# Causal attention in a four-layer kernel: scores and maxima over one head's 32 rows, the mask added by VectorE, keys and queries turned two groups ahead

## The chip, the cores and the metric

One NeuronCore of a Trainium2 chip runs the whole program. Its engines are TensorE (PE in the profile; PEld is its loading of weights), VectorE (DVE), ScalarE (ACT), GpSimd (POOL) and SyncE (SP, which here only issues transfers). The metric is the device time of one execution in microseconds, the median over several.

## The reference

The input `x` is 4 batches of 1024 tokens of 128 values. Four layers follow one another, each added to `x`: attention, a feed-forward layer with 8 experts, a second attention-like layer with a sigmoid, and the feed-forward layer again. The change is in the first:

```
k, q, v = (x @ Wk, @ Wq, @ Wv) as 16 heads of 8 values;  k, q = layernorm over the 8
dot  = einsum('bqhs,bkhs->bhqk', q, k) / sqrt(8);  dot = where(causal, dot, -inf)
attn = softmax(dot);  out = einsum('bhqk,bkhs->bqhs', attn, v) @ Wo + bo
```

## The kernel before

A batch has 8 tiles of 128 tokens, and its 16 heads are 4 groups of 4 heads. So attention is a row of 16 groups, numbered G = 4 b + g. A head has 32 rows on the partitions, four heads fill the 128. Its 8 values are stored as a rounded part and a rest, so that products of rounded numbers (fp32r) are exact enough: rows 0 to 7 and 8 to 15 of a key hold the rounded value, 16 to 23 the rest; two more rows hold ones in the keys and, in the queries, minus the maximum of the row (again as two parts); the others are zero. One matmul thus gives the score minus the maximum, and the exponential needs nothing more.

For every group there are two passes over queries times keys:

- **Maxima** (`maxima_unit` in TensorE, L704, mask L707; in VectorE L1208): queries on the partitions, up to 512 keys as columns. VectorE reduces each to one column. Where the diagonal tile is the last, a bf16 matmul of the identity with a mask adds a large negative number above the diagonal. Queries over 512 have two parts, and their two maxima are joined in `shift` (L1216). `shift` writes minus the maximum into the queries' two rows, which are then turned again (`turn_low`, `turn_high`) into `qmT`.
- **Scores** (`scores` L719; ScalarE's `weights` L894): keys on the partitions, up to 512 queries as columns. ScalarE takes the exponential into `prob`, POOL's `keep` (L1034, L1036) zeroes what lies below the diagonal of a diagonal tile, and TensorE's `weigh` (L737) multiplies with the values: four heads side by side, 128 rows by 32 columns each, into `o_acc`. ScalarE reads it out once a group (`empty_out`, L899).

In both passes the matmul is over all 128 rows. That one head alone counts is reached by `k_apart`: a copy of the turned keys for each head in which the other heads' rows are zero. SyncE's `spread` (L628) makes it with four transfers a group, after the keys `kT` are there; the zeros are written once by POOL (L254 in setup, L1105).

Everything is laid out by hand. `sequence` yields the steps of a group in one order and every engine walks the same order, doing its own part and counting the others'. Each unit of work (a score unit, a maxima unit, a turn of four tiles, a projection) takes the next of six PSUM banks in a ring: TensorE waits until the bank's last reader is through, the reader until the unit is full. A group has 38 score units and 39 maxima units. The scores are those of group G, the maxima those of G + 1: they begin in the tenth score step and end in the 37th. The steps between are placed by `PLACE`, a list of 24 score numbers. Queries of G + 1 are turned at its start and emptied by VectorE (L1258), keys of G + 2 near its end and emptied by ScalarE (L888). Group 1 of a batch also projects the next batch (L686), group 2 normalises its keys and queries (POOL's `square` and `affine`, L998 to L1008), group 0 finishes the batch before. In the last five groups come steps of the feed-forward layer's routing, and POOL sends rows by indirect transfers (`send`, L1068) in the last two.

The opening makes the first batch's projections, turns the first keys and queries, and runs all maxima of group 0 with nothing beside them.

## Time and profile before

| | us |
|---|---|
| median of the timed runs | 2882.5 (2881.8 to 2883.1) |
| profiled execution: span from first to last instruction | 2834.4 |
| what lies around the span, if that execution took the median | 48.1 |
| attention's groups: first maximum, last reading of `o_acc` | 42.5, 724.3 |
| one plain group (198.3 to 234.0) | 35.7 |
| a group that projects the next batch (278.9 to 320.9) | 42.0 |
| a group that normalises it (320.9 to 360.5) | 39.6 |
| mean granted TensorE clock | 0.97 |

The profiled execution is known by its span; 48.1 us is the median less the span. A group is measured from one reading of `o_acc` (L899) to the next, sixteen in all. Two matmuls may overlap: the duration of one (its mean ns) holds the way through the array, and the time from one start to the next is what a stream of them costs. Busy time counts overlapping instructions once.

### The profile page before, as it was taken

How to read it: one execution, taken by the hardware profiler on the slowest of the kernel's cores; microseconds unless marked ns; L12 is line 12 of the kernel's file. 1: busy time of each engine (PE TensorE's matmuls, PEld its weight loads, DVE VectorE, ACT ScalarE, POOL GpSimd, SP SyncE). 2: the span in 40 equal slices, each digit the busy share in tenths (PEclk: the TensorE clock that was granted, in tenths of full speed). 3: DMA queues.
4: the chain of work that ended last, by engine and by line, in shares of the span. 5: the costliest groups of instructions: out<-in, count | busy, mean ns of one | idle time of the engine just before them, and what ended most of it. 6: DMA issues, size and time to landing. Idle time of an engine off the chain costs nothing. (4 is left out here: it accounts for less than half of the span.)

```text
span 2834.4 us, 54508 instructions
## 1 busy us (share of the span) xinstructions
PE 2635.7 (93%) x19182; PEld 1713.2 (60%) x19182; DVE 1789.9 (63%) x3491; ACT 1578.4 (56%) x2843; POOL 820.0 (29%) x1181
## 2 busy tenths in 40 slices
PE   5999998998689979999999999999999999996997
PEld 3555565655478845666555665555555555554886
DVE  7777777786466745555665556555556655555666
ACT  2666666666454455555555556555566555554443
POOL 4142422525345311111111111112121123322642
PEclk8999999999799979999999999999999999997998
DMA  6500000001424258888878888887888788885222
GB/s 109 82 16 16 8 16 16 16 9 31 119 83 157 94 130 196 195 196 196 204 184 200 196 196 189 190 187 177 188 189 190 183 201 200 206 199 203 71 87 85
DMA packets 190430, 383.21 MB, mean 135 GB/s; under 512 B 45281, under 2 KB 100714, under 8 KB 188810
## 3 DMA queue, kind: packets, MB, share of 16 engines
q1 hardware_dynamic: 181578, 362.55, 53.9%
q0 software_dynamic: 8640, 17.84, 1.8%
q8 instruction: 132, 2.16, 0.4%
q14 instruction: 80, 0.66, 0.1%
HBM read 38.10 MB, written 39.86 MB: 28 GB/s over the span
## 5 line engine op out<-in xcount | busy, mean ns | idle before, releaser
L3050 DVE STREAM_TRANSPOSE m_turned<-m_sig 128x1024 f32<-128x1024 f32 x512 | 613.6, 1227 | 429.5 <-ACT m_sig L2820 201.1
L2643 PE MATMUL m_v_ps<-m_sig,m_tok 128*64 128x512 f32 x2048 | 468.2, 599 | 0.0
L2656 PE MATMUL m_v_ps<-m_sigT,m_tok 128*64 128x256 f32 x4064 | 461.5, 380 | 3.2 <-DMA m_sigT<-m_turned 3.2
L1208 DVE TENSOR_REDUCE a_maxima<-a_bank 128x1 f32<-128x512 f32 (+4 forms) x624 | 367.4, 643 | 121.1 <-PE a_bank L707 73.2
L2627 PE MATMUL m_f_ps<-m_swap,m_own 64*128 64x512 f32 x1536 | 426.2, 404 | 15.6 <-DMA m_swap<-m_own 7.4
L894 ACT ACTIVATE a_prob<-a_bank 128x512 f32<-128x512 f32 (+1 forms) x608 | 322.2, 586 | 201.0 <-PE a_bank L719 197.5
L2627 PE MATMUL m_f_ps<-m_own,m_swap 64*128 64x512 f32 x1536 | 426.4, 404 | 0.0
L2656 PEld LDWEIGHTS m_v_ps<-m_sigT,m_tok 128*64 128x64 f32 x4064 | 289.4, 137 | 200.3 <-issue 54.8
L2916 POOL TENSOR_TENSOR m_own<-m_uv,m_own 128x1024 fp32r<-128x1024 f32 x64 | 152.0, 2375 | 813.4 <-ACT m_own L2782 813.4
L2820 ACT ACTIVATE m_sig<-m_f_ps 128x1024 f32<-128x1024 f32 x256 | 248.3, 1022 | 245.4 <-issue 147.5
L2627 PEld LDWEIGHTS m_f_ps<-m_swap,m_own 64*128 64x128 f32 x1536 | 271.6, 186 | 99.9 <-ACT m_sig L2806 25.8
L2643 PEld LDWEIGHTS m_v_ps<-m_sig,m_tok 128*64 128x64 f32 x2048 | 135.8, 137 | 265.3 <-issue 265.0
L719 PE MATMUL a_bank<-a_qmT,k_apart 128*128 128x512 f32 (+3 forms) x768 | 266.0, 407 | 25.0 <-DVE a_maxima L1208 11.6
L2806 ACT ACTIVATE m_sig<-m_f_ps 128x512 f32<-128x512 f32 x512 | 264.2, 603 | 41.0 <-PE m_f_ps L2627 39.3
L2627 PEld LDWEIGHTS m_f_ps<-m_own,m_swap 64*128 64x128 f32 x1536 | 271.4, 186 | 5.6
L704 PE MATMUL a_bank<-k_apart,a_qT 128*128 128x512 f32 (+3 forms) x768 | 249.2, 386 | 26.2 <-DVE a_maxima L1208 11.6
L2832 ACT CAST m_v1T_hi<-m_v_ps 128x256 fp32r<-128x256 f32 x128 | 47.7, 372 | 276.9 <-PE m_v_ps L2656 272.5
L719 PEld LDWEIGHTS a_bank<-a_qmT,k_apart 128*128 128x128 f32 x768 | 131.5, 197 | 97.9 <-issue 64.0
L704 PEld LDWEIGHTS a_bank<-k_apart,a_qT 128*128 128x128 f32 x768 | 146.6, 202 | 61.9 <-DVE a_maxima L1208 24.4
L3059 DVE TENSOR_TENSOR m_v1T_lo<-m_v_ps,m_v1T_hi 128x256 fp32r<-128x256 f32 x128 | 54.2, 424 | 204.5 <-ACT m_v1T_hi L2832 204.3
L737 PE MATMUL a_o_acc<-a_prob,v 128*32 128x512 f32 (+3 forms) x1536 | 147.4, 501 | 9.6 <-POOL a_prob L1036 7.5
L1827 PE MATMUL f_y_ps<-f_w_down,f_innerT 128*128 x1136 | 150.3, 275 | 1.4 <-DVE f_y_rows L2237 1.1
(509 smaller groups left out, 4268.6 us busy)
## 6 DMA issues: line engine op xcount, KB each, us to landing
m_sigT<-m_turned SPq DMA_DIRECT2D x2042, 128.0 KB, 2.3
m_swap<-m_own SPq DMA_DIRECT2D x64, 256.0 KB, 3.2
f_t_rows<-f_sent_rows SPq DMA_DIRECT2D x142, 65.0 KB, 2.1
f_sent_rows<-a_proj SPq DMA_DIRECT2D x34, 260.0 KB, 9.5
k_apart<-a_kT SPq DMA_DIRECT2D x64, 128.0 KB, 2.4
m_swap<-m_own SPq DMA_DIRECT2D x64, 128.0 KB, 3.2
f_h<-back_rows SPq DMA_DIRECT2D x8, 512.0 KB, 5.6
rows<-back_rows SPq DMA_DIRECT2D x6, 512.0 KB, 4.9
```

The costliest lines, as they stand in the source:

```text
L704: mm = pe.matmul(out[:, i, :], qT[g % 2][:, qt * P:(qt + 1) * P], k_apart[g % 2][:, h + i, k0:k1], start=(i == 0 or not masked), stop=not ...
L719: mm = pe.matmul(out[:, i, :], k_apart[g % 2][:, h + i, j * P:(j + 1) * P], qmT[g % 2][:, q0:q1], start=True, stop=True)
L894: act.activation(prob[j % 2][:, h:h + heads, prob_cols(j, q0, q1)], src, ACT.Exp).then_inc(u.free(), 1)
L1208: dve.tensor_reduce(maxima[:, qt, h:h + heads, part], src, AX.X, ALU.max).then_inc(u.free(), 1)
L1827: mm = pe.matmul(y_ps[:, 0:DIM], innerT[p][:, ib * P:(ib + 1) * P], w_down[:, ds(e * INTER + ib * DIM, DIM)], start=(ib == 0), stop=(ib == ...
L2627: mm = pe.matmul(f_ps[s][:, cols], tile_of(u[rows, :], j + s * SIDE), v[rows, cols], start=start, stop=stop)
L2643: mm = pe.matmul(v2_ps[h * RANK:(h + 1) * RANK, :], tok[p][:, 0, j + s * SIDE, :], sig[j % 2][s][:, h * HALF:(h + 1) * HALF], start=(j == ...
L2656: mm = pe.matmul(v1_ps[h * RANK:(h + 1) * RANK, g * 2 * P:(g + 1) * 2 * P], tok[p][:, 1, jj, :], sigT[g][:, :, 2 * h:2 * h + 2, jj, :].rea ...
L2806: ins = act.activation(sig[1][s][:, cols], f_ps[s][:, cols], ACT.Sigmoid)
L2820: act.activation(sig[j % 2][s][:, :], f_ps[s][:, :], ACT.Sigmoid).then_inc(sig_ready, 1)
L2916: pool.tensor_tensor(own_lo[p][:, :], uv32[:, :], own_hi[p][:, :].bitcast(F32), ALU.subtract).then_inc(lo_ready, 1)
L3050: dve.transpose(turned[g][:, :, q, :, :], sig[j % 2][s][:, :].rearrange("p (t j a) -> p j t a", j=4, a=STACK)).then_inc(turn_ready, 1)
```

## The change

- `k_apart`, its clearing and its transfers go. Scores and maxima read the 32 rows of one head straight from `kT`, `qT` and `qmT`, so each matmul is 32 rows by 128 columns. A unit holds one head's pieces, one or two tiles' worth; unit n of the scores has head n mod 4, of the maxima (n + 2) mod 4.
- The mask matmuls go. `mask` is 128 x 512 in fp32, zero but for its last 128 columns, and VectorE's `tensor_tensor_reduce` adds it and takes the maximum in one instruction, with the first part's maximum (`first_max`) as its start value. It also writes the masked scores, into four buffers that nobody reads.
- Keys are kept in three buffers, and both keys and queries are turned two groups ahead, near a group's end. ScalarE empties them and `qmT`'s second half, where VectorE did.
- 40 score units and 40 maxima units; maxima run from the first score step to the 38th. `PLACE` is gone, the steps are placed by score numbers. `prob` is laid out by a table, and two diagonal tiles share a unit in two places.

```diff
-        SCORES, MAXES = list(score_units()), list(max_units())
+        SCORE_PIECES = (((0, 0, HALF),), ((1, P, HALF),), ((0, HALF, SEQ),), ((1, HALF, SEQ),), ((2, 2 * P, HALF), (3, 3 * P, HALF)),
+                        ((2, HALF, SEQ),), ((3, HALF, SEQ),), ((4, 4 * P, SEQ),), ((5, 5 * P, SEQ),), ((6, 6 * P, SEQ), (7, 7 * P, SEQ)))
+        MAX_PIECES = (((0, 0, P), (1, 0, 2 * P)), ((2, 0, 3 * P),), ((3, 0, HALF),), ((4, 0, HALF),), ((5, 0, HALF),),
+                      ((4, HALF, 5 * P), (5, HALF, 6 * P)), ((6, 0, HALF),), ((6, HALF, 7 * P),), ((7, 0, HALF),), ((7, HALF, SEQ),))
+        SCORES = [(pieces, h) for pieces in SCORE_PIECES for h in range(GROUP)]
+        MAXES = [(pieces, (h + GROUP // 2) % GROUP) for pieces in MAX_PIECES for h in range(GROUP)]
-        WEIGHED_AFTER = {LAST_OF[1]: (0,), LAST_OF[2]: (1,), LAST_OF[3]: (2,), LAST_OF[4]: (3,), LAST_OF[6]: (4, 5)}
+        WEIGHED_AFTER = {15: (0,), 20: (1,), 27: (2,), 32: (3,), 36: (4,), 39: (5,)}
...
         def sequence(g, prev, prep, follows, stage=None):
-            begin, end, made = PLACE[4], 36, 0
-            if prev and follows:
-                yield "spread", 0
+            two_ahead, first = prep or g < HALVES_OF, follows and not prev
+            begin, end, made = 6 if first else 0, 37, 0
...
+                if two_ahead and i in (31, 32, 34, 35):
+                    yield ("keys", "queries")[i // 34], (31, 32, 34, 35).index(i) % HALVES_OF
...
+                if prep and g == 2 and i in (0, 2, 5, 7, 9, 10, 12, 20, 21):
+                    yield {0: ("square", 1), 2: ("square", 0), 5: ("square_sums", 0), 7: ("head_dev", 0), 9: ("head_rstd", 0),
+                           10: ("affine", 1), 12: ("stack_keys", 0), 20: ("affine", 0), 21: ("stack_queries", 0)}[i]
...
         @block.tensor
+            def maxima_unit(u, G, n, stacks=()):
+                pieces, h = MAXES[n]
+                out, rows, col = u.next(), head_rows(h), 0
                 u.wait_empty(pe, *stacks)
-                if n == 0:
-                    pe.wait_ge(k_spread, 16 * GROUP * (G + 1))
-                for i in range(heads):
-                    mm = pe.matmul(out[:, i, :], qT[g % 2][:, qt * P:(qt + 1) * P], k_apart[g % 2][:, h + i, k0:k1], start=(i == 0 or not masked), stop=not masked)
-                if masked:
-                    mask = k["mask"][:, :].unsqueeze(1).broadcast_to([P, heads, P])
-                    mm = pe.matmul(out[:, :, k1 - k0 - P:k1 - k0], k["ident16"][:, :], mask, start=False, stop=True)
+                for qt, k0, k1 in pieces:
+                    mm = pe.matmul(out[:, col:col + k1 - k0], qT[G % 2][rows, qt * P:(qt + 1) * P], kT[G % KEPT_KEYS][rows, k0:k1], start=True, stop=True)
+                    col += k1 - k0
                 mm.then_inc(unit_full, 1)
...
-                for i in range(heads):
-                    mm = pe.matmul(out[:, i, :], k_apart[g % 2][:, h + i, j * P:(j + 1) * P], qmT[g % 2][:, q0:q1], start=True, stop=True)
+                for j, q0, q1 in pieces:
+                    mm = pe.matmul(out[:, col:col + q1 - q0], kT[G % KEPT_KEYS][rows, j * P:(j + 1) * P], qmT[G % 2][rows, q0:q1], start=True, stop=True)
...
         @block.vector
+            def maxima_unit(u, n, firsts_made, masked_by):
+                pieces, h = MAXES[n]
+                src, col = u.next(), 0
                 u.wait_full(dve)
-                dve.tensor_reduce(maxima[:, qt, h:h + heads, part], src, AX.X, ALU.max).then_inc(u.free(), 1)
+                masks = any(k1 == (qt + 1) * P for qt, _, k1 in pieces)
+                if masks:
+                    masked_by.append(u.n)
+                    if len(masked_by) > MASKED_OUTS:
+                        u.wait_emptied(dve, masked_by[-1 - MASKED_OUTS])
+                for qt, k0, k1 in pieces:
+                    width = k1 - k0
+                    scores, first = src[:, col:col + width], first_max[:, qt % HALF_T, h:h + 1]
+                    masked = masked_out[(len(masked_by) - 1) % MASKED_OUTS][:, col:col + width]
+                    col += width
+                    if k1 < (qt + 1) * P:
+                        ins = dve.tensor_reduce(first, scores, AX.X, ALU.max)
+                        firsts_made[qt, h] = u.n
+                        continue
+                    if k0:
+                        u.wait_emptied(dve, firsts_made[qt, h])
+                    ins = dve.tensor_tensor_reduce(out=masked, in0=scores, in1=k["mask"][:, HALF - width:HALF], scale=1.0,
+                                                   scalar=first if k0 else MASKED, op0=ALU.add, op1=ALU.max, accum_out=maxima[:, qt, h:h + 1])
+                ins.then_inc(u.free(), 1)
```

## Rows read from the trace of the kernel before

**Rows 1.** The page's first part: busy us, share of the span, instructions of each engine.
```profile
PE 2635.7 (93%) x19182; PEld 1713.2 (60%) x19182; DVE 1789.9 (63%) x3491; ACT 1578.4 (56%) x2843; POOL 820.0 (29%) x1181
```
**Rows 2.** Table of stretches: length, busy us (instructions) by engine, clock, DMA share, GB/s.
```profile
42.00:70.00 28.00, 22.38 (x89) 14.18 (x89) 24.94 (x45) 2.22 (x3) 14.50 (x19) 0.80 1.10 157
70.00:695.80 625.80, 580.56 (x3902) 362.94 (x3901) 474.10 (x997) 393.81 (x764) 213.01 (x384) 0.97 0.12 23
278.90:320.90 42.00, 41.60 (x276) 26.20 (x274) 27.09 (x52) 27.23 (x62) 7.41 (x18) 0.98 0.06 13
320.90:360.50 39.60, 36.80 (x249) 22.40 (x249) 31.10 (x56) 25.10 (x47) 24.98 (x32) 0.96 0.06 14
360.50:396.10 35.60, 33.90 (x240) 20.70 (x238) 26.42 (x50) 22.12 (x43) 9.09 (x24) 1.00 0.07 16
617.40:661.80 44.40, 38.55 (x252) 23.07 (x251) 38.07 (x103) 28.00 (x60) 6.42 (x17) 0.96 0.06 13
695.80:724.30 28.50, 18.86 (x138) 8.74 (x137) 1.00 (x4) 15.06 (x30) 20.96 (x32) 0.88 0.12 38
```
**Rows 3.** Groups by line and shape, 198.3 to 234.0: count, busy us, mean ns, idle before.
```profile
L1208 DVE TENSOR_REDUCE a_maxima<-a_bank 128x1 f32<-128x512 f32 x24 | 15.1, 684 | 4.3 <-PE a_bank L704 2.5 <-PE a_bank L707 1.8
L1208 DVE TENSOR_REDUCE a_maxima<-a_bank 128x1 f32<-128x384 f32 x8 | 4.3, 555 | 0.6 <-PE a_bank L707 0.5
L1258 DVE CAST a_qT<-a_bank 128x512 fp32r<-128x512 f32 x2 | 1.3, 684 | 1.4 <-PE a_bank L668 1.4
```
**Rows 4.** Stretch 198.3 to 234.0 of L1208, L707 and L737 alone, in this order.
```profile
198.30:234.00 35.70, 22.97 (x40) 1.00 0.07 16
198.30:234.00 35.70, 5.82 (x24) 2.26 (x24) 1.00 0.07 16
198.30:234.00 35.70, 8.98 (x96) 2.46 (x96) 1.00 0.07 16
```
**Rows 5.** TensorE in order of time, around 300 us: start, us, instruction.
```profile
299.75 0.40 PE L704 MATMUL a_bank<-k_apart,a_qT 128*128 128x512 f32 x1
300.08 1.50 PE L737 MATMUL a_o_acc<-a_prob,v 128*32 128x256 f32 x16
...
303.37 0.39 PE L719 MATMUL a_bank<-a_qmT,k_apart 128*128 128x512 f32 x1
303.60 0.60 PE L668 MATMUL a_bank<-ident,k_st 128*128 128x128 f32 x4
...
304.25 0.48 PE L719 MATMUL a_bank<-a_qmT,k_apart 128*128 128x512 f32 x1
304.57 0.34 PE L704 MATMUL a_bank<-k_apart,a_qT 128*128 128x384 f32 x1
```
**Rows 6.** TensorE in order of time at 1500 us, the second attention layer's 64-row matmuls.
```profile
1500.57 0.39 PE L2627 MATMUL m_f_ps<-m_swap,m_own 64*128 64x512 f32 x1
1500.57 0.39 PE L2627 MATMUL m_f_ps<-m_own,m_swap 64*128 64x512 f32 x1
1500.81 0.39 PE L2627 MATMUL m_f_ps<-m_swap,m_own 64*128 64x512 f32 x1
```
**Rows 7.** VectorE: five reductions in order of time; then groups of the whole span.
```profile
213.23 3.08 DVE L1208 TENSOR_REDUCE a_maxima<-a_bank 128x1 f32<-128x512 f32 x5 [0.84 <-PE a_bank L704]
...
L2280 DVE TENSOR_TENSOR f_inner<-f_silu,f_up 128x512 f32<-128x512 f32 x142 | 97.7, 688 | 39.5 <-PE f_up L1805 20.7 <-ACT f_silu L1958 15.8 <-PE f_out L1814 2.4
L2246 DVE SCALAR_TENSOR_TENSOR x<-f_h,ratio,x 128x128 f32<-128x128 f32 x32 | 11.0, 343 | 0.0
L2237 DVE COPY f_raw<-f_y_ps 128x128 f32<-128x128 f32 x96 | 27.9, 291 | 39.3 <-PE f_y_ps L1827 37.8 <-issue 0.6
```
**Rows 8.** Setup and the opening in order of time.
```profile
8.08 3.54 POOL L255 MEMSET k_st<- 128x4096 f32 x1
8.20 3.44 DVE L90 TENSOR_SCALAR a_spread<-a_spread 128x8 f32<-128x8 f32 x1
...
38.06 0.59 ACT L888 CAST a_qT<-a_bank 128x512 fp32r<-128x512 f32 x1 [0.27 <-PE a_bank L668]
...
41.57 0.66 PE L704 MATMUL a_bank<-k_apart,a_qT 128*128 128x128 f32 x2 [3.54 <-DMA k_apart<-a_kT]
```

More of the change, by code:

```diff
@@ L341, in attention_phase @@
     HEAD_STAGES, EARLY_UNITS = 5, 12
+    KEPT_KEYS, MASKED_OUTS = 3, 4
     with ExitStack() as ctx, ExitStack() as phase:
@@ new lines, in sequence @@
+                if prev and i == 17:
+                    for n in range(HALVES_OF):
+                        yield "turn_out", n
+                if prev and g == 0 and i in (23, 29):
+                    for n in range(HALVES_OF):
+                        yield ("turn_tokens", "project_out")[i == 29], n
+                if prep and g == 1:
+                    if i in (1, 3, 5):
+                        yield ("token_stats", "token_dev", "token_norm")[i // 2], 0
+                    if i in (13, 15):
+                        yield "turn_z", i // 15
+                    if i in (21, 23, 26, 29):
+                        for n in range(2):
+                            yield "project", 2 * (21, 23, 26, 29).index(i) + n
@@ L554, in sequence @@
+                if prev and g == 0 and 32 <= i <= 36:
+                    yield ("add_x", 0) if i == 32 else ("out_stats", i - 33)
+                if follows and i == 21:
+                    yield "turn_low", 0
                 if stage is not None:
@@ L599, in head_rows @@
             return slice(h * STACK, (h + 1) * STACK)
-        def by_head(bank, width, heads):
-            return bank[:, 0:heads * width].rearrange("p (i w) -> p i w", w=width)
         def half_of(tile, n):
@@ L890, in weights @@
             def weights(u, n):
-                j, h, heads, q0, q1 = SCORES[n]
-                src = by_head(u.next(), q1 - q0, heads)
+                pieces, h = SCORES[n]
+                src, width = u.next(), sum(q1 - q0 for _, q0, q1 in pieces)
+                to, off = prob_of(*pieces[0][0:2])
+                start = pieces[0][1] - off
                 u.wait_full(act)
-                act.activation(prob[j % 2][:, h:h + heads, prob_cols(j, q0, q1)], src, ACT.Exp).then_inc(u.free(), 1)
+                act.activation(to[:, h, start:start + width], src[:, 0:width], ACT.Exp).then_inc(u.free(), 1)
             def empty_out(G):
@@ L1387, in early_table, with group @@
                 dve.tensor_scalar(k["early_expert"][:, :], expert_sum[0:1, :], -1.0, None, ALU.add)
[L1389 to L1391 removed]
+            def group(u, link, b, g, prev, prep, follows, masked_by, head_made=()):
+                ahead, projected, firsts_made = (g + 1) % GROUPS, [], {}
                 for what, n in sequence(g, prev, prep, follows, stage_of(b, g)):
                     if what == "max":
[L1394 to L1395 removed]
+                        made = maxima_unit(u, n, firsts_made, masked_by)
+                    elif what == "next_keys":
+                        keep_turned(u, half_of(kT[(GROUPS * b + ahead) % KEPT_KEYS], n))
+                    elif what == "next_queries":
                         keep_turned(u, half_of(qT[ahead % 2], n))
[L1397 to L1401 removed]
                     elif what == "shift":
@@ L1411, in group @@
                         out_stats(b - 1, n)
-                    elif what in ("score", "keys", "turn_low", "turn_tokens", "turn_z", "project"):
+                    elif what in ("score", "keys", "queries", "turn_low", "turn_high", "turn_tokens", "turn_z", "project"):
                         u.next()
```

255 lines of the change are left out of this document (81 added, 174 removed).

## The prediction

> **What bounds the kernel now.** I read the page's first part first: TensorE is busy 93% of the span, VectorE 63%, ScalarE 56% [rows 1]. That is a mean over stages, so the table of stretches comes next. The change touches attention alone, and attention's pipeline of sixteen head groups runs from 42 us (first maximum) to 724 us (last reading of the output bank). Between 70.0 and 695.8 us TensorE is busy 580.6 of 625.8 us (0.93), VectorE 474.1 (0.76), ScalarE 393.8 (0.63) [rows 2]. The reader is to see there that TensorE is the full engine in attention, but that VectorE stands only 107 us behind it: whatever is taken from TensorE brings gain only until VectorE is full. Two stretches are different. In the opening (42 to 70 us) there are only maxima, and VectorE is busy 24.9 of 28.0 us (0.89). In the last group (695.8 to 724.3) there are no maxima, VectorE is idle, and POOL has 21.0 of 28.5 us, its row transfers standing between the diagonal masks for which the weighing waits [rows 2].
>
> Third, one plain group, 198.3 to 234.0 us, by line and by shape. It takes 35.7 us. VectorE's maxima cost 22.97 us of it, the mask matmuls 5.82 us, the weighing 8.98 us [rows 4]; a maximum over 512 columns takes 684 ns, over 384 columns 555 ns, an eviction by VectorE 684 ns [rows 3].
>
> **The change, part by part.**
>
> Mask matmuls out of TensorE. 23 units a group end in one, 5.82 us of busy time [rows 4]. Part of that lies beside neighbours; on the other hand a 512-column matmul behind one is followed after 0.32 us (304.25 to 304.57) and without one after 0.23 us (303.37 to 303.60) [rows 5]. I take 5.0 us a group.
>
> Scores and maxima over 32 rows. Their columns are as many as before: 2 x 18,432 a group (4 heads x 4,608), or 72 matmuls' worth of 512 columns, at 0.23 us each 16.6 us [rows 5]. Neighbouring units use different 32-row strips. The trace has no 32-row strips, but it has 64-row ones: two matmuls of 64 x 512 start together and the next two 0.24 us later [rows 6], so a pair costs what one costs. Bounds for the 16.6 us: no overlap (0 saved) and four at once (12.4 saved). I take half, 8.3 us, the row being pairs.
>
> Changes of shape. A weighing (128 x 32) that follows a 512-column matmul starts 0.33 us after it, instead of 0.23 [rows 5]: about 0.1 us a change. The turns (128 x 128), eight or more a group, now stand between 32-row matmuls, so up to 16 changes more, plus the lost overlap: +1.8 us (bounds 0 and 4). The Trainium skill (TensorEngine Tiling (Array Packing), Key Properties) says that a change of tiling mode drains TensorE; the trace's 0.1 us agrees, and without a price on the page the sum goes by the row.
>
> TensorE in all, over the 15 groups of the long stretch: 580.6 - 15 x 5.0 + 15 x 1.8 - 15 x 8.3 = 408 us. It stops being the bound.
>
> VectorE's maxima. Columns stay (18,432), instructions go from 39 to 48 a group, 16 plain and 32 that add the mask from SBUF, take the maximum and write both. Start to start a 512-column reduction costs (3.08 - 0.69) / 4 = 0.60 us [rows 7], and by 129 ns for 128 columns [rows 3] about 0.08 us of that doesn't depend on width. Nine more instructions are +0.7 us, less what the by-unit busy count already holds of gaps: +0.4. The masked form is not in this trace. From below: a two-input sum of 512 columns with one input in PSUM takes 688 ns, as the reduction does (0 more); one with an operand read per partition takes 343 ns against 291 for a copy of the same 128 columns (+0.05) [rows 7]. From above: half rate, worked out as a rival. I take +0.055 us for 32 instructions, 1.8 us. The maxima become 22.97 + 0.4 + 1.8, near 25.2 us. The Trainium skill (VectorE: DVE Perf Modes, Two Vector instructions with no wait between them) says that an instruction which also writes its accumulator is two, the second a read of the accumulator; no run here shows it, and it would put the addition above my value, by the cost of a small instruction.
>
> Evictions moved. Two of qT and one of qmT go from VectorE to ScalarE: -3 x 0.60 = -1.8 us for VectorE, +3 x 0.59 [rows 3, 8] for ScalarE. The maximum of the two parts over 16 columns goes too (-0.2). VectorE's sum: +2.2 - 2.0, nothing. ScalarE has 393.8 + 15 x 2 = 424 us and stays third.
>
> Order. Maxima now run from the first score to the 38th, where they began at the tenth; VectorE's idle stretch at the head of a group goes. What is late next is VectorE itself, and then TensorE's bursts: a weighing of about 1.5 us [rows 5] lets VectorE's share of the six banks (three, 1.8 us of work) run dry for about 0.7 us, four times a group. Keys and queries two groups ahead are waited for in good time, except in the group that normalises the next batch, where POOL has 25 us of work [rows 2] (a rival).
>
> The spread. 64 transfers and the wait for them go. They cost where nothing else runs: once, in the opening. The last cast of the queries ends at 38.65 us and the first maximum's matmul starts at 41.57 [rows 8]: -2.9 us. Against it the opening's maxima, which are VectorE's, take 2.2 us more. In setup the cleared 4,096 columns of POOL go. VectorE's tiny instruction L90 lasts 3.44 us, exactly beside POOL's second clearing (8.08 to 11.62 us), and ScalarE waits for it [rows 8]. That clearing starts at 4.9 now: -3.0 us, with 0.3 for the wider mask counted.
>
> **Sum.** What share can VectorE reach when it is the bound? 0.89 in the opening, where nothing disturbs it, and 0.857 in the stretch from 617.4 to 661.8 us, where TensorE has nearly as much to do [rows 2]. I take 0.87: 474 / 0.87 = 545 us. The three groups that project the next batch (as 278.9 to 320.9 [rows 2]) don't get there: TensorE has 41.6 - 5.0 + 1.8 - 8.3 = 30.1 us, ScalarE 29, so 33.5 instead of 31.1: +7. Together 552 against 625.8: -74. The last group is POOL's: 0. Opening -0.7, setup -3.0. Nothing behind attention changes. Total -78 us of the execution's 2834.4 us span; the timed runs have a median of 2882.5, 48 us more, for what lies around the span, and I carry the difference over: 2805 us.
>
> **Rivals.**
> Masked maxima at half rate (slower). 10,240 of a group's columns go through the masked form; at 1.01 ns each [rows 3] half rate costs 10.3 us a group instead of 1.8. VectorE: 474 + 15 x 8.5 = 602 us; at a share of 0.91 (between 0.89 and TensorE's 0.93 now) 661 us, 35 over today's, and with the opening's 8.5 - 0.7 and setup's -3 about +40: 2922 us. It decides from the point where VectorE's group grows by (625.8 x 0.87 - 474) / 15 = 4.7 us, 0.2 us per masked instruction. Against it: every two-input row of the trace runs at full rate [rows 7]. The Trainium skill (Vector Engine (DVE) Microarchitecture Reference, Points that are easy to get wrong) names half throughput for an accumulating form with two wide SBUF sources; here one source is PSUM. Chance 0.09.
>
> Strips don't overlap. TensorE then has 533 us; at 0.93 that is 573, with VectorE at 0.83 beside it rather 578: -48, so 2831 us. Rows 6 speak against it. Chance 0.13.
>
> The clock. Where TensorE is not full it is granted less: mean 0.80 in the opening, 0.88 in the last group, 1.00 in a full group [rows 2]. At 0.88 its 408 us become 464, still under VectorE's, but every burst is longer, some 1.5 us a group: -55, 2828 us. Chance 0.14; that it stays at half for good, and TensorE becomes the bound again at 816 us, 0.02 (far slower), since a full TensorE is shown at full clock.
>
> POOL late in the group of 25 us of work (its diagonal masks stand behind its scaling steps): 3 us in three batches, 2814 us. Chance 0.08.
>
> **Numbers.** Forecast 0.54, rivals as given. Lower end: VectorE at TensorE's share of today, 474 / 0.93 = 510, -119: 2764. Upper end: the rivals of 2828 and 2831 together, 2855. Half rate is left out. What a measurement tells from no change is 0.2%, 6 us. Faster 0.87 (all but half rate and the dead clock), slower 0.11, same 0.02 (a price near 0.2 us per masked instruction).
>
> **What would show it.** Groups of 30 to 31 us where they took 35.7, VectorE at 0.87 or more there and TensorE under 0.8; the masked form at 0.65 us for 512 columns start to start; pairs of 32-row matmuls starting within a few ns of each other after a weighing; a mean clock near 1 in full groups; the first maximum about 6 us earlier. A masked form above 0.8 us, or a clock below 0.9, would make it wrong.

## The result and the profile after

The changed kernel takes 2941.2 us (median of five; 2907.5 to 2947.5) against 2881.8 us for the kernel before in the same session: 1.019 times the time, 95% interval 1.014 to 1.024. It is slower by about 59 us where 77 us less were forecast, and outside the range. Four of the five runs lie at 2940 to 2947 us; the profiled one is the fifth, of 2907.5 us (span 2905.7). A second set, taken later, gave 2924.8 us and a ratio of 1.014 [1.009, 1.019], with a profiled span of 2931.5 us; its trace is called after2 below. The two sets differ in size, not in sign.

The page's first part for the kernel after, and three rows of its second (the span in 40 slices), against [rows 1]:

```profile
PE 2671.1 (92%) x18814; PEld 1641.2 (56%) x18814; DVE 1784.2 (61%) x4087; ACT 1597.3 (55%) x2918; POOL 811.9 (28%) x1179
...
PE   6988998999678979999999999999999999996897
...
DVE  7677677667364755555665556555556655556556
...
PEclk7688877767899989999999999999999999997998
```

TensorE has 368 instructions fewer and yet 35 us more busy time, and it is still the full engine in attention (the first ten slices). What has changed there is the third line: 6 to 8 tenths of the full clock, where the long stretch before had 0.97 [rows 2].

Stretches of the kernel after (columns as in rows 2): up to the last read of the attention's output; the opening; a plain group; then three stretches at a single level of the clock.

```profile
0.00:756.60 756.60, 668.36 (x3816) 325.15 (x3816) 526.31 (x1704) 446.05 (x907) 259.10 (x457) 0.76 0.11 20
...
36.00:70.00 34.00, 28.68 (x79) 16.07 (x79) 28.64 (x89) 5.52 (x10) 16.84 (x22) 0.55 1.25 181
...
207.20:243.00 35.80, 34.48 (x226) 15.81 (x224) 26.28 (x89) 23.11 (x48) 8.86 (x24) 0.86 0.00 1
...
613.40:657.60 44.20, 42.41 (x187) 21.27 (x185) 29.38 (x96) 24.40 (x47) 12.26 (x23) 0.50 0.00 1
252.00:278.50 26.50, 25.37 (x188) 14.02 (x186) 22.97 (x79) 17.61 (x37) 6.54 (x18) 1.00 0.01 1
463.50:493.50 30.00, 29.45 (x198) 14.61 (x190) 18.80 (x64) 20.81 (x51) 5.48 (x13) 1.00 0.01 2
```

In 613.4 to 657.6 us the granted clock is at its lower level (1.2 of 2.4 GHz) throughout, while TensorE is busy 42.41 of 44.20 us. "Busy" doesn't mean "at full clock". The trace of the kernel before has such a stretch too, though short: TensorE busy all the time, at the lower level.

```profile
328.13:331.54 3.41, 3.41 (x17) 1.24 (x9) 2.21 (x2) 1.31 (x3) 0.00 (x0) 0.50 0.00 0
```

A clock of 0.76 over 756.6 us, with only two levels, is (1 - 0.76) x 2 x 756.6 = 363 us at the lower one; summed from the trace's own record it is 365.1 us, against 70.6 us before the last read in the kernel before (its second profile, before2 below). The sum over all stretches of the kernel after at the upper level, from 70.0 to 728.4 us:

```profile
sum 347.19, PE 332.43 PEld 173.83 DVE 263.94 ACT 243.67 POOL 114.25; mean PE 17.50 PEld 9.15 DVE 13.89 ACT 12.82 POOL 6.01
```

So even at full clock TensorE is busy 0.96 of the time and VectorE 0.76. The forecast had under 0.8 for the one and 0.87 for the other.

The next rows are groups of TensorE's instructions in the stretch 252.0 to 278.5 us (upper level):

```profile
L640 PE MATMUL a_bank<-a_qmT,a_kT 32*128 32x512 f32 x16 | 5.5, 493 | 0.2
L627 PE MATMUL a_bank<-a_kT,a_qT 32*128 32x512 f32 x13 | 4.9, 446 | 0.0
L660 PE MATMUL a_o_acc<-a_prob,v 128*32 128x512 f32 x32 | 4.2, 595 | 0.0
```

and these the same three in 613.4 to 657.6 us (lower level): 754, 779 and 1030 ns for 446, 493 and 595.

```profile
L627 PE MATMUL a_bank<-a_kT,a_qT 32*128 32x512 f32 x17 | 11.3, 754 | 1.1 <-DVE a_maxima L1155 1.0
L640 PE MATMUL a_bank<-a_qmT,a_kT 32*128 32x512 f32 x17 | 10.3, 779 | 0.0
L660 PE MATMUL a_o_acc<-a_prob,v 128*32 128x512 f32 x40 | 9.1, 1030 | 0.0
```

VectorE's work is as forecast. By shape, 207.2 to 243.0 us (the answer to rows 3 and 4):

```profile
L1150 DVE TENSOR_REDUCE a_first_max<-a_bank 128x1 f32<-128x512 f32 x16 | 10.3, 684 | 4.8 <-PE a_bank L627 4.7
L1155 DVE CUSTOM_DVE_ANT_0 a_masked_out<-a_bank,mask 128x512 f32<-128x512 f32 x5 | 3.2, 685 | 0.0
L1155 DVE CUSTOM_DVE_ANT_0 a_masked_out<-a_bank,mask,a_first_max 128x512 f32<-128x512 f32 x4 | 2.9, 750 | 1.0 <-PE a_bank L627 1.0
L1155 DVE DVE_READ_ACCUMULATOR2_ANT a_maxima<- 128x1 f32 x32 | 2.6, 83 | 0.0
```

The masked form runs at the plain reduction's rate (685 against 684 ns for 512 columns); the read of the accumulator behind it costs 83 ns, the start value read per partition 65 ns. All the maxima of the group are 25.0 us, against 22.97 before [rows 4]: the stretch by VectorE's instructions of L1150 alone, then of L1155 alone.

```profile
207.20:243.00 35.80, 10.29 (x16) 0.86 0.00 1
...
207.20:243.00 35.80, 14.72 (x65) 0.86 0.00 1
```

The setup and the opening of the kernel after in order of time (before: L90 3.44 us, first matmul of a maximum at 41.57 us, [rows 8]):

```profile
8.52 0.34 DVE L90 TENSOR_SCALAR a_spread<-a_spread 128x8 f32<-128x8 f32 x1
...
36.62 0.67 PE L627 MATMUL a_bank<-a_kT,a_qT 32*128 32x128 f32 x10 [0.77 <-ACT a_qT L814]
...
38.05 0.23 DVE L1155 CUSTOM_DVE_ANT_0 a_masked_out<-a_bank,mask 128x128 f32<-128x128 f32 x1
```

### The profile page after: what moved, and what is told of

It reads as the page before. It is cut to its first block and busy times, and to the rows that moved or that the text cites. A ratio compares the mean times of both kernels' runs of the same rounds, so it can differ in the third digit from the quotient of the medians.

```text
span 2905.7 us, 54730 instructions
## 1 busy us (share of the span) xinstructions
PE 2671.1 (92%) x18814; PEld 1641.2 (56%) x18814; DVE 1784.2 (61%) x4087; ACT 1597.3 (55%) x2918; POOL 811.9 (28%) x1179
## 5 line engine op out<-in xcount | busy, mean ns | idle before, releaser
L2573 PE MATMUL m_f_ps<-m_swap,m_own 64*128 64x512 f32 x1536 | 426.0, 404 | 16.6 <-DMA m_swap<-m_own 8.4
L627 PE MATMUL a_bank<-a_kT,a_qT 32*128 32x512 f32 (+3 forms) x768 | 277.6, 496 | 31.8 <-DVE a_maxima L1155 20.2
L640 PE MATMUL a_bank<-a_qmT,a_kT 32*128 32x512 f32 (+3 forms) x768 | 247.0, 501 | 25.9 <-DVE a_maxima L1155 13.2
L1150 DVE TENSOR_REDUCE a_first_max<-a_bank 128x1 f32<-128x512 f32 x256 | 165.1, 684 | 91.8 <-PE a_bank L627 89.4
L640 PEld LDWEIGHTS a_bank<-a_qmT,a_kT 32*128 32x128 f32 x768 | 112.4, 220 | 167.5 <-issue 110.5
L660 PE MATMUL a_o_acc<-a_prob,v 128*32 128x512 f32 (+3 forms) x1536 | 198.1, 639 | 5.9 <-POOL a_prob L968 3.6
L627 PEld LDWEIGHTS a_bank<-a_kT,a_qT 32*128 32x128 f32 x768 | 138.1, 226 | 108.4 <-DVE a_maxima L1155 50.2
L3005 DVE TENSOR_TENSOR m_v1T_lo<-m_v_ps,m_v1T_hi 128x256 fp32r<-128x256 f32 x128 | 54.2, 423 | 217.0 <-ACT m_v1T_hi L2778 205.6
L1773 PE MATMUL f_y_ps<-f_w_down,f_innerT 128*128 x1136 | 153.3, 278 | 25.8 <-DVE f_raw L2183 17.9
```

The source lines that it names most:

```text
L627: mm = pe.matmul(out[:, col:col + k1 - k0], qT[G % 2][rows, qt * P:(qt + 1) * P], kT[G % KEPT_KEYS][rows, k0:k1], start=True, stop=True)
L640: mm = pe.matmul(out[:, col:col + q1 - q0], kT[G % KEPT_KEYS][rows, j * P:(j + 1) * P], qmT[G % 2][rows, q0:q1], start=True, stop=True)
L660: mm = pe.matmul(o_acc[h * STACK:(h + 1) * STACK, q0:q1], v1[:, j, g * GROUP + h, :], weights_at[:, h, q0 - off:q1 - off], start=(j == 0), ...
L1150: ins = dve.tensor_reduce(first, scores, AX.X, ALU.max)
L1773: mm = pe.matmul(y_ps[:, 0:DIM], innerT[p][:, ib * P:(ib + 1) * P], w_down[:, ds(e * INTER + ib * DIM, DIM)], start=(ib == 0), stop=(ib == ...
L2573: mm = pe.matmul(f_ps[s][:, cols], tile_of(u[rows, :], j + s * SIDE), v[rows, cols], start=start, stop=stop)
```

## The experiments

All the numbers are from the table; the text under each heading says what it decides. "Last read" is the start of the last copy of the attention's output bank. "Lower level" is the time before it that the trace's record of the granted clock has at 1.2 GHz. "Rest" is the last read less half of the lower level: the time that would be left if everything in those stretches ran twice as fast. It is an estimate and a lower bound, since VectorE's and ScalarE's work doesn't. "Pairs" counts, between 70 and 760 us, a scores and a maxima matmul that follow one another in order of time and start within 20 ns of each other, of some 1,480 such matmuls. Two scores or two maxima matmuls are not counted. In onestrip and fill2 the attention ends later, so that the count covers a part of it, and fill2's takes in its added matmuls. Ratios are to the kernel before in the same session, with 95% intervals.

```
kernel      median us  ratio                  last read  lower level  rest   pairs
before2     2875.0     (one run)               726.3       70.6      691.0     0
after       2941.2     1.019 [1.014, 1.024]    756.6      365.1      574.0   307
after2      2924.8     1.014 [1.009, 1.019]    785.3      419.3      575.6   310
rows128     2840.9     0.987 [0.985, 0.988]    693.2       95.6      645.4     0
rows64      2883.9     1.002 [1.001, 1.003]    733.1      215.0      625.6   226
fill2       3010.9     1.046 [1.044, 1.048]    857.6      331.9      691.7   385
samestrip   2890.4     1.004 [1.002, 1.006]    739.8      340.7      569.4   367
alldiffer   2872.8     0.998 [0.996, 0.999]    722.4      290.2      577.3   489
onestrip    3059.4     1.064 [1.062, 1.067]    902.7      587.1      609.2     0
pairs       2875.1     0.999 [0.998, 1.000]    728.5      218.2      619.4   257
twice       2873.3     0.999 [0.997, 1.000]    719.3       61.4      688.6     0
apart2      2868.1     0.996 [0.994, 0.997]    718.4       90.2      673.3     0
apartb      2840.5     0.986 [0.984, 0.987]    694.0       75.1      656.5     0
```

**rows128**: the changed kernel with all 128 rows in every scores and maxima matmul.

```diff
-                out, rows, col = u.next(), head_rows(h), 0
+                out, rows, col = u.next(), slice(0, P), 0
...
-                link(dve.tensor_scalar(hi.bitcast(F32R), maxima[:, mine, :], -1.0, None, ALU.mult))
+                link(dve.tensor_scalar(hi.bitcast(F32R), maxima[:, mine, :], -0.25, None, ALU.mult))
```

(The first edit stands in `maxima_unit` and in `scores`, the second in both instructions of `shift`. rows64 is edited at the same places, onestrip at the first alone. All three leave out that the heads are kept apart: they time the same instructions, but don't compute the attention.)

> The changed kernel, but scores and maxima read all 128 rows (the four heads' scores are summed, and minus a quarter of the maximum stands in each head, so the softmax stays in range; the heads are not kept apart, that part of the computation is changed). Instructions, columns, banks and order are those of the changed kernel; only the rows of 80 matmul units a group differ. Clock theory (a matmul over 32 rows does not keep TensorE's clock up): mean granted clock of 0 to 760 us back from 0.76 to 0.94 or more, plain groups 32 to 34 us, 2800 to 2840 us in all. Rival (what costs is the changes of shape and the drains between 32-row and 128-column work): also faster, but by 1.6 us a group, to about 2880 us, with the clock still under 0.85. Rival (VectorE's masked maxima are the cost): no change, 2905 to 2945 us.

Measured: 2840.9 us, 84 to 100 us under the changed kernel's two sets, with columns, units, waits and VectorE's instructions as they were. Its row up to the last read:

```profile
0.00:693.20 693.20, 613.25 (x3816) 384.43 (x3816) 525.54 (x1704) 447.73 (x906) 260.36 (x457) 0.93 0.11 21
```

VectorE has the same 526 us as in the kernel after; the clock is 0.93 instead of 0.76. So VectorE isn't what lost the time. TensorE was idle as much in both, 48 of 596 us here and 57 of 658 us in the kernel after (70 us to the last read but one), so that gaps in its work don't tell the two apart either.

**rows64**: the same with the rows of two heads.

```diff
+                out, rows, col = u.next(), slice(h // 2 * 2 * STACK, (h // 2 * 2 + 2) * STACK), 0
```

> As before it, but each matmul reads the 64 rows of two heads (two heads' scores summed, minus half of the maximum in each). Clock theory, if what counts is the rows in use: clock between those of 32 and 128 rows, 0.85 to 0.93 in attention, 2830 to 2890 us; it keeps the overlap of two strips, so it could also equal 128 rows. Shape rival: like 32 rows, 2905 to 2945 us, since a 64-row matmul changes the shape as often.

Measured: 2883.9 us, 215 us at the lower level: between 32 and 128 rows in both. With 32, 64 and 128 rows in use the lower level has 365, 215 and 96 us. A 64-row matmul changes the array's shape as often as a 32-row one, so the rival of the changes of shape doesn't account for the 150 us between them.

**fill2**: an extra matmul of 128 rows and 512 columns ahead of every second maxima unit.

```diff
+                if n % 2 == 0:
+                    pe.matmul(out[:, 0:HALF], qT[G % 2][:, pieces[0][0] * P:(pieces[0][0] + 1) * P], kT[G % KEPT_KEYS][:, 0:HALF], start=True, stop=True)
```

> The changed kernel with work added: before every second maxima unit one matmul of 512 columns over all 128 rows, into the same bank, overwritten by the unit's own. 20 a group, at 0.23 us and two changes of shape (0.1 us each) 8.6 us a group at full clock. Clock theory: the clock in attention rises to 0.9 or more, and the kernel with more work is faster than without, 2840 to 2900 us. Shape and VectorE rivals: the added work is paid, +60 to +130 us, 2990 us or more.

Measured: 3010.9 us. The 320 fillers took the lower level down by 33 us only (365 to 332) and put 118 us into the rest (574 to 692), 0.37 us each. Full-row work bought for its own sake costs more than the clock gives back. The clock theory's forecast (a clock of 0.9 or more in attention, 2840 to 2900 us) failed: the share of the time at the lower level fell from 0.48 to 0.39 only. The time that came is the one its rivals had named, 2990 us or more. The rows in use thus move the clock the way the theory says, but no run gives a rule for how much.

**samestrip**: the heads of the maxima in another order.

```diff
-        MAXES = [(pieces, (h + GROUP // 2) % GROUP) for pieces in MAX_PIECES for h in range(GROUP)]
+        MAXES = [(pieces, h) for pieces in MAX_PIECES for h in range(GROUP)]
```

> The changed kernel with the maxima's heads in the scores' order, so that a score unit and the maxima unit beside it use the same 32 rows and cannot overlap; four neighbours of one kind still differ. If overlap of strips carries much of the time (the prediction took 8.3 us a group): 20 us or more above the changed kernel. If banks come free one by one and TensorE is late only in bursts: within 15 us of it.

Measured: 2890.4 us, 34 to 51 us faster than the changed kernel. The premise was wrong: in the order of the steps, scores unit n is followed by maxima unit n + 1 in the first half of a group and n + 2 in the second, and then by scores unit n + 1. So in the changed kernel's order (h + 2) a maxima unit has the strip of the scores unit ahead of it in the second half, and in this order that of the scores unit behind it in the first: each order has one neighbour on the same strip in one half. This one came out with more overlaps (367 against 307), not none; why more isn't shown. Two places of the kernel after, where the strips are the same (0.33 us apart) and where they differ (together):

```profile
299.86 0.49 PE L640 MATMUL a_bank<-a_qmT,a_kT 32*128 32x512 f32 x1
300.19 0.39 PE L627 MATMUL a_bank<-a_kT,a_qT 32*128 32x128 f32 x2
...
532.94 0.79 PE L627 MATMUL a_bank<-a_kT,a_qT 32*128 32x512 f32 x1
532.94 0.68 PE L640 MATMUL a_bank<-a_qmT,a_kT 32*128 32x384 f32 x1
```

**before2**: no edit.

> The kernel before once more, for a second trace of it. Its first profiled execution had a span of 2834.4 us, while the timed ones lay at 2873 to 2882; the 44 us between them would lie in what follows the attention, 2110 us there and 2146 to 2151 us in the five other kernels' traces. If the first profile was one short execution: this one shows a span near 2878, its last read of the attention's output near 724 us, and some 2150 us behind it. If instead a profiled execution of this kernel always runs short: a span near 2834 again, and 2110 us behind.

Measured: span 2873.2 us, last read 726.3. What follows the last read, in the profile that the prediction was read from and in this one:

```profile
724.30:2834.40 2110.10, 1996.44 (x14998) 1314.36 (x14998) 1260.75 (x2383) 1154.65 (x2012) 552.33 (x722) 0.97 0.70 171
```

```profile
726.30:2873.20 2146.90, 2000.65 (x14998) 1312.91 (x14998) 1257.57 (x2383) 1150.55 (x2012) 552.38 (x722) 0.98 0.68 168
```

The first profiled execution was a short one, by 37 us, all but 2 of it behind attention with the same instructions. The twelve other traces of the study have 2146 to 2153 us there. A timed run is 1.8 us above its span, not the 48 us that the prediction carried over as lying around the span.

**onestrip**: every scores and maxima matmul on the rows of head 0.

```diff
+                out, rows, col = u.next(), head_rows(0), 0
```

> The changed kernel with every scores and maxima matmul on the rows of head 0 (the heads are not kept apart, so what is computed is not the attention asked for; columns, units and all waits are as in the changed kernel). No two neighbours are ever on different strips, so none overlap. Theory (TensorE's clock follows how many rows are in use at a time, and half of the pairs overlapped before): less work at a time, so the clock stays at its lower level for longer than the changed kernel's 365 us, and the overlaps are gone: at full clock 8.3 us a group more, at half 16.6; 15 groups at 8 to 20 us more make 3060 to 3200 us. Rival (the overlap is too seldom to matter and the clock is already set by one strip's rows): within 20 us of the changed kernel's 2941.

Measured: 3059.4 us, just under the theory's 3060 to 3200, and no overlaps. The row up to the last read:

```profile
70.00:902.70 832.70, 806.17 (x3682) 462.61 (x3681) 488.43 (x1555) 452.36 (x862) 231.42 (x413) 0.67 0.01 4
```

TensorE is busy 97% of the stretch and the clock is at 0.67, the lowest of the study: with matmuls of 32 rows one at a time the lower level came oftener than with those that overlap. The rival (within 20 us of 2941) is out.

**alldiffer**: maxima and scores beside each other on different strips all through a group.

```diff
+        MAXES = [(pieces, (h + (i < 5)) % GROUP) for i, pieces in enumerate(MAX_PIECES) for h in range(GROUP)]
```

> The changed kernel with the heads' order of the maxima such that a maxima unit and the scores unit beside it are on different strips all through a group (in the changed kernel only in the first half; the order alone is changed). Theory (rows in use at a time): 16 more pairs a group overlap, 4 us a group at full clock, and the clock keeps its upper level longer: 2850 to 2900 us, and less than 300 us at the lower level before the attention's last read. Rival (what differs between orders is chance in where the lower stretches fall): between 2890, the one other order run so far, and 2941.

Measured: 2872.8 us, 489 pairs, 290 us at the lower level. One line of order takes 52 to 68 us off the changed kernel and brings it to the time of the kernel before, a little under it. The rest is the same in samestrip, after and alldiffer (569 to 577 us); what differs is the lower level. So of the theory's two parts one failed: 182 more pairs than in the kernel after took nothing off the rest, where 4 us a group were expected, and all of the gain came by the clock.

**apart2**: the changed kernel's order of work and its masking, with the former matmuls over 128 rows.

```diff
-    KEPT_KEYS, MASKED_OUTS = 3, 4
+    KEPT_KEYS, MASKED_OUTS = 2, 4
-            begin, end, made = 6 if first else 0, 37, 0
+            begin, end, made = 9, 37, 0
...
+                    mm = pe.matmul(out[:, col:col + k1 - k0], qT[G % 2][:, qt * P:(qt + 1) * P], k_apart[G % 2][:, h, k0:k1], start=True, stop=True)
...
+                    ins = dve.tensor_tensor_reduce(out=scores, in0=scores, in1=k["mask"][:, HALF - width:HALF], scale=1.0,
```

> The changed kernel's order of work, its masking within VectorE's maximum and its turns two groups ahead, but with the kernel before's matmuls over all 128 rows (keys spread to two zeroed buffers by SP at a group's start; maxima begin at step 9 of 40, since the buffer is only then free and filled; VectorE writes the masked scores back to their bank, and the mask is in bf16). The full attention is computed. Theory (the 32-row matmuls alone cost the time; the rest of the change is worth what rows128 showed, 39 us): 2835 to 2860 us, the clock at its lower level for about 100 us of the attention, a group without projections at 31 to 35 us. Rival (the maxima all through a group were what made rows128 fast, and begun at step 9 they queue on VectorE): 2865 to 2885 us.

Measured: 2868.1 us, in the rival's range (2865 to 2885) and outside the theory's. The clock is as the theory had it, 90 us at the lower level. Here three quarters of the rows of each key buffer are zero, as in the kernel before: rows of zeros kept the clock up as other rows did. Part of the time is a price that I had added: with the masked scores written back to their bank, and the mask in bf16, the read of the accumulator takes 144 ns instead of 83.

```profile
L1190 DVE DVE_READ_ACCUMULATOR2_ANT a_maxima<- 128x1 f32 x480 | 68.9, 144 | 0.0
L1190 DVE CUSTOM_DVE_ANT_0 a_bank<-a_bank,mask,a_first_max 128x512 f32<-128x512 f32 x60 | 43.0, 756 | 4.0 <-PE a_bank L667 3.9
L1190 DVE CUSTOM_DVE_ANT_0 a_bank<-a_bank,mask 128x512 f32<-128x512 f32 x60 | 41.1, 722 | 19.7 <-PE a_bank L667 19.6
```

**pairs**: matmuls over two heads' 64 rows, one head's zeroed, on three spread buffers, in alldiffer's order.

```diff
+        def pair_rows(h):
+            return slice(h // 2 * 2 * STACK, (h // 2 + 1) * 2 * STACK)
...
+                    sp.dma_start(k_apart[G % APARTS][rows, h % 2, :].bitcast(F32), kT[G % KEPT_KEYS][rows, :].bitcast(F32)).then_inc(k_spread, 16)
```

> The changed kernel with scores and maxima over two heads' 64 rows, the other head's rows zeroed (SP spreads each group's keys to one of three buffers of two slots, right after they are turned, four DMAs of 128 KB that took 2.4 us each in apart2), and the heads' order of alldiffer, so that most neighbouring units stand on different halves of the rows and can overlap. Masking, turns two groups ahead and maxima all through a group stay; the full attention is computed. Theory (the time is the work at full clock, which overlapping shortens, plus half of what is spent at the lower level, which more rows in use shorten): alldiffer spent 290 us at the lower level before the attention's last read, rows64 215, rows128 96; with overlapping pairs of 64 rows under 180, and the work at full clock between alldiffer's 577 and rows64's 626 us; 2810 to 2850 us. Rival (64-row matmuls on different halves don't overlap, as rows64's time suggests): 2870 to 2890, rows64's 2884. Other rival (the spread of keys lands too late for maxima that begin with the group): 1 to 3 us a group more than the theory.

Measured: 2875.1 us. Halves do overlap (257 pairs), but hardly oftener than in rows64 (226), and the lower level has the same 218 us. The first maximum comes at 42.6 us, as before the change. The forecast of 2810 to 2850 failed: the pairs that the order should bring didn't come, and the lower level stayed over the 180 us expected. The time lies in the first rival's range (2870 to 2890), but its reason doesn't hold, since halves do overlap. Why there are few pairs isn't shown. TensorE waited for the spread once between 70 and 700 us, for 1.1 us, so the other rival is out.

**twice**: rows128 with TensorE's mask matmul put back; the heads are not kept apart here either.

```diff
+                    if masked:
+                        mm = pe.matmul(out[:, col - P:col], k["ident16"][:, :], k["mask16"][:, :], start=False, stop=True)
```

> rows128 (scores and maxima over all 128 rows, the clock near full) with TensorE's mask matmul put back in every masked piece of a maxima unit, 32 of 128 columns a group, while VectorE masks as well (masking twice changes nothing): the mask matmuls' price on TensorE by itself. Theory (my sum took 5.0 us a group for them, TensorE being the bound): 16 groups at 4 to 5 us, 2905 to 2921 us against rows128's 2841. Rival (TensorE waits for VectorE's maxima in rows128, so the matmuls fit beside): under 20 us more, below 2861.

Measured: 2873.3 us, 32 us over rows128. The mask matmuls have 110.1 us of busy time, 7.3 us a group, but TensorE's busy time grew by 34 us only: the remainder of each lies beside a neighbour. The answer is between the theory (64 to 80) and the rival (under 20). With the mask matmuls the lower level is shorter, 61 us against 96. The group, then the stretch of twice and that of rows128:

```profile
L634 PE MATMUL a_bank<-mask,ident 128*128 128x128 bf16 x477 | 110.1, 233 | 0.0
```

```profile
70.00:719.30 649.30, 600.63 (x4152) 369.13 (x4151) 475.00 (x1552) 435.20 (x859) 232.18 (x413) 0.97 0.02 5
```

```profile
70.00:693.20 623.20, 566.71 (x3668) 353.26 (x3667) 471.72 (x1544) 428.19 (x857) 231.91 (x412) 0.95 0.02 5
```

**apartb**: apart2 with three places mended.

```diff
-    KEPT_KEYS, MASKED_OUTS = 2, 4
+    KEPT_KEYS, MASKED_OUTS = 2, 3
-            begin, end, made = 9, 37, 0
+            begin, end, made = 5, 37, 0
+        masked_out = [sb(f"a_masked_out{i}", [P, HALF], BF16) for i in range(MASKED_OUTS)]
-        o_tokT = sb("a_o_tokT", [P, SEQ])
+        o_tokT = oT
-            pool.memset(k["k_apart0"][:, :, :].bitcast(F32), 0.0)
+            for i in range(2):
+                pool.memset(k[f"k_apart{i}"][:, :, :].bitcast(F32), 0.0).then_inc(other_cleared, 1)
```

(The last edit moves the clearing from the setup to POOL's part behind it. The mask is in f32 again, too.)

> apart2 (128-row matmuls on spread keys, masking in VectorE, turns two groups ahead; the full attention) with three places mended: VectorE writes the masked scores to a buffer of 512 bf16 columns in SBUF instead of back to their bank (in apart2 the read of the accumulator behind it took 144 ns against 83 in the changed kernel, and the 512-column form 722 against 685: about 3 us of VectorE a group), the two 3.5 us clearings of the key buffers stand behind the setup on POOL (apart2's first maximum came at 42.6 us, the changed kernel's at 38.2), and the maxima begin at step 5 instead of 9. Theory (each of these was on the path): 4.4 us at the opening and 0.5 to 1.3 us in each of 15 groups, so 2845 to 2857 us, the attention's last read near 700. Rival (only TensorE's work and clock count, 673 us of work at full clock in apart2): the opening's 4 us alone, 2862 to 2866. Other rival (the spread, 2.4 us and its issue, is late for step 5): 2868 or more.

Measured: 2840.5 us, 0.986 [0.984, 0.987] of the kernel before and 2.9% under the changed one (2924.8 in the same session), with the whole attention computed: the version that beats both. It came out 5 us under the theory. The edits came together, so what each is worth isn't shown, and with them stays open how much of apart2's time was the late start of the maxima, its rival's cause. Two groups of VectorE by shape:

```profile
L1197 DVE DVE_READ_ACCUMULATOR2_ANT a_maxima<- 128x1 f32 x480 | 39.6, 82 | 0.0
L1197 DVE CUSTOM_DVE_ANT_0 a_masked_out<-a_bank,mask 128x512 bf16<-128x512 f32 x60 | 38.4, 686 | 1.9 <-PE a_bank L667 1.5
```

and the long stretch:

```profile
70.00:694.00 624.00, 568.24 (x3690) 354.18 (x3688) 470.18 (x1557) 432.86 (x864) 232.90 (x415) 0.96 0.12 25
```

The accumulator's read is back at 82 ns, the clock at 0.96, near the 0.97 before the change [rows 2].

**after2**: no edit, beside the same runs of before as apartb.

> The changed kernel once more, beside the same runs of the kernel before: its first profile was of an execution of 2907 us, while its timed ones lay at 2940 to 2947. Theory (where the lower clock falls decides, and it falls differently from one execution to the next): the time at the lower level before the attention's last read comes out other than 365 us by about twice the difference in time; an execution of 2940 would show near 430. Rival (the executions differ in what follows the attention, as those of the kernel before did): the last read near 757 us again, and more behind it.

Measured: span 2931.5 us, 25.8 over the first profile, and the last read is 28.7 us later with 54.2 us more at the lower level, 0.53 us each. What follows the last read is 2146 us against 2149. Nor is it these two alone: in the nine timed runs of the changed kernel the mean granted clock is 0.920 in the two shortest and 0.906 to 0.909 in the five longest, and span times clock, the time that two levels leave at full clock, is 2661 to 2678 us, while the spans go from 2906 to 2946. Most of the changed kernel's spread is the spread of its time at the lower level.

## Why the prediction was wrong

**The step that failed: the clock, put at nothing "since a full TensorE is shown at full clock".** The prediction gave the clock two cases: 2828 us at 0.88 (0.14), and "that it stays at half for good, and TensorE becomes the bound again at 816 us, 0.02 (far slower), since a full TensorE is shown at full clock". That reason was read from rows in which every scores and maxima matmul had 128 rows, and it was a mean: the stretch from 328.13 to 331.54 us, shown above, is full and at the lower level. The changed one's have 32, and in 613.4 to 657.6 us TensorE is full and at the lower level. What happened lies between the two cases: mean clock 0.76, or 0.73 in after2. The price by the table: the lower level grew from 71 to 365 us, (365 - 71) / 2 = 147 us, against 117 us won in the rest (691 to 574): +30, which is the last read's 726.3 to 756.6. Between its two cases the prediction had given the clock no chance. That the rows in use are the cause is shown by the edits to the rows alone (rows128, rows64, onestrip) and that overlap matters by the edits to the order alone (samestrip, alldiffer). How it comes about in the chip, and how many rows are enough, stay open. The Trainium skill (TensorE: Matmul & The Clock Gate, HAM oscillation) puts such changes of clock down to gaps in TensorE's work. The kernel before agrees: seven of the eight falls of its clock between 70 us and the last group came in or just behind a gap of 2.2 us or more. In the kernel after only two of eighteen did, and a stretch of 44.2 us at the lower level has TensorE busy 96%; there the measurement decides.

**TensorE's 408 us: "it stops being the bound".** This failed too, apart from the clock. Busy time at the upper level plus half of that at the lower, between 70 us and the last read but one, is 467 us in the kernel after against 563 in before2: an estimate of the work at full clock. 96 us went, where the prediction took 580.6 - 408 = 172. From 252.0 to 278.5 us VectorE does reach 0.87, the share that the forecast gave it as the bound, but from 463.5 to 493.5 us, at full clock as well, it has 18.80 of 30.00 us and TensorE 29.45, and over all stretches at the upper level 0.76 against 0.96. Busy time counts a matmul's way through the array, so this doesn't prove TensorE the bound everywhere; it does show that VectorE was not full. That the rest, itself an estimate, fell by 117 us all the same, more than the 78 us forecast, is therefore not the prediction's mechanism come true.

**Mask matmuls, 5.0 us a group.** Mis-sized, by what can be measured beside 128-row matmuls. twice against rows128 has 32 us for 16 groups, 2.0 us each; by the rest, with the lower level taken out, 43 us, 2.7 each. I took the busy time (5.82 us) less a little; the increase in TensorE's busy time was 34 us over 15 groups, 2.3 each.

**Strips, half of the 16.6 us.** The mechanism is right: on different strips two start in the same 10 ns. The count was off. "Neighbouring units use different 32-row strips" held for all neighbours in the first half of a group only. Half of the 16.6 us would need 740 of 1,481 matmuls to start with the one before; 307 did so as a scores and a maxima matmul, and 545 with two of one kind counted too. The rest of rows128 less that of the changed kernel is 71 us, 4.5 a group against 8.3. The 1.8 us a group for changes of shape are in this difference, and no run separates them.

**VectorE.** Right: a group's maxima take 25.0 us where 25.2 were forecast, and VectorE's busy time before the last read is 526 us against 530 in before2. But the size came right by luck. The addition itself is free; the 1.8 us taken for it stand where the accumulator's reads are (83 ns each, 2.6 us a group), which the sum didn't have, and the start values. The rival of half rate is refuted at 685 ns.

**The opening and the setup.** The setup's gain came as taken: ScalarE's L206, behind L90, at 8.89 us instead of 11.67, 2.8 for 3.0. The spread's wait gave less: the first matmul of a maximum came 4.95 us earlier in all (36.62 against 41.57), so 2.2 for 2.9, and the first maximum 4.5 us (5.1 in after2) where "about 6" was forecast. None of it was kept. The opening's clock fell from 0.80 [rows 2] to 0.55, the rows being a part of it only (rows128 has 0.65 from 36 to 70 us), and the first read of the output bank came at 121.5 us (116.1 in after2) against 115.3.

**Behind attention.** Nothing changed, as said (2146.9 us in before2, 2149.1 after). The 48 us "around the span" was wrong, and harmless only because it was carried over as a constant.

The forecast signs "groups of 30 to 31 us" and "mean clock near 1 in full groups" both failed: 35.8 us and 0.86 in the plain group above. So did "TensorE under 0.8". The sign that named this outcome was the last one, "or a clock below 0.9, would make it wrong".

## What to carry to other kernels

A matmul that uses a quarter of the rows is not a cheaper matmul with the same clock: before taking a full engine's clock as given, ask whether the instructions that fill it stay the same. Read "busy" beside the granted clock, stretch by stretch, and where TensorE is full reckon the lower level at about half its length (0.53 between two executions here). Where small-row matmuls are used all the same, set the order so that neighbours stand on different strips, which cost one line here and was worth 52 to 68 us, and keep the rest of such a change (masking within the maximum, maxima all through a group), which was worth 1.4% with full rows.

## What the runs showed of the hardware

- With the same columns, the time at the lower level before the last read was 96 us with 128 rows, 215 with 64, 365 to 419 with 32, and 587 with 32 and no overlap. Other orders of the same 32-row matmuls had 341 and 290 us.
- Rows of zeros in the keys counted as rows in use: with 128 rows, three quarters of them zero, the lower level was 71 to 90 us (before2, apart2, apartb), and with 64 rows, half of them zero, 218 us against 215 without zeros (pairs, in another order, and rows64).
- An accumulator's read took 83 ns behind a masked maximum that wrote to SBUF and 144 ns behind one that wrote to PSUM; the 512-column form took 685 and 722 ns. The second had its mask in bf16 as well, and no run separates the two. In the first a start value read per partition added 57 to 65 ns.
- An output in bf16 left the masked form's rate alone: 686 ns for 512 columns in apartb, 685 in the changed kernel with an f32 output.
- VectorE's tiny L90 took 3.44 us beside POOL's clearing of 4,096 columns and 0.34 us right after it.
- Two executions of one kernel differed by 37 us with the same instructions behind attention (2110 and 2147 us).
